# Second attention: each head's scores on one half of the array's rows, a second copy of the negated maxima, late scores last

## The reference

```
q = (x @ wq).reshape(b, s, H, HD)        # H = 32, HD = 16
k = (x @ wk).reshape(b, s, H, HD)
v = (x @ wv).reshape(b, s, H, HD)
q = _apply_rotary(q, cos, sin)
k = _apply_rotary(k, cos, sin)
scores = jnp.einsum('bqhd,bkhd->bhqk', q, k) * scale
scores = jnp.where(causal[None, None], scores, jnp.finfo(scores.dtype).min)
probs = jax.nn.softmax(scores, axis=-1)
out = jnp.einsum('bhqk,bkhd->bqhd', probs, v).reshape(b, s, d)
return out @ wo
```

## Time and profile before

| | before |
|---|---|
| median of 3 runs | 1991.2 us (1982.42 to 1991.51) |
| profiled execution, its own time | 1992.31 us |
| its span | 1990.6 us |
| mean granted TensorE clock | 0.984 |
| TensorE busy | 1926.6 us (97%) |
| weight loads busy | 1688.1 us (85%) |
| VectorE busy | 1504.9 us (76%) |
| ScalarE busy | 883.7 us (44%) |
| GpSimd busy | 908.0 us (46%) |

### The profile page before, as it was taken

One profiled execution on the slowest core, in us unless ns is written; L12 is line 12 of the kernel. 1 busy time (PEld: TensorE's weight loads), 2 busy tenths in 40 slices (PEclk: granted clock), 3 DMA queues, 4 the chain that ended last, 5 costly groups with the idle time before them and its releaser, 6 DMA issues.

```text
span 1990.6 us, 41276 instructions
## 1 busy us (share of the span) xinstructions
PE 1926.6 (97%) x13992; PEld 1688.1 (85%) x13992; DVE 1504.9 (76%) x2322; ACT 883.7 (44%) x2235; POOL 908.0 (46%) x872
## 2 busy tenths in 40 slices
PE   8999979999999999999999999988999989999998
PEld 3688869999999999999999999987888868888776
DVE  2577657887788788877887788888888457778886
ACT  1233334444444444444444444446554346666432
POOL 0133354444444444444444444454684557777111
PEclk9999989999999999999999999999999889999999
DMA  9577741111111111111111111411487754443121
GB/s 342 170 242 243 236 143 42 47 48 47 48 47 47 48 47 46 41 44 42 47 47 48 47 47 43 141 43 64 141 245 210 220 164 137 140 135 112 38 64 58
DMA packets 197085, 207.20 MB, mean 104 GB/s; under 512 B 18554, under 2 KB 167930, under 8 KB 195996
## 3 DMA queue, kind: packets, MB, share of 16 engines
q1 hardware_dynamic: 196156, 205.53, 33.5%
q10 hardware_dynamic: 864, 0.79, 0.1%
HBM read 126.43 MB, written 71.43 MB: 99 GB/s over the span
## 4 chain that ended last, share of the span: by engine, by line
PE 77%; issue 11%; DVE 5%; POOL 3%; SPq 2%; DMA 2%; ACT 1%; POOLq 0%; DVEq 0%; ACTq 0%
PE ps L1036 18%; PE ps L997 18%; PE ps L1011 7%; PE ps L1025 4%; PE ps L1048 4%; PE ps L2128 3%; PE ps L1020 3%; PE ps L2099 3%; PE ps L2557 2%; POOL k_rot L570 2%; PE ps L1806 2%; PE ps L2148 2%; PE ps L2521 2%; PE ps L1118 1%; PE ps L1814 1%
## 5 line engine op out<-in xcount | busy, mean ns | idle before, releaser
L1036 PE MATMUL ps<-wo,ot 128*128 (+1 forms) x1536 | 389.0, 402 | 0.0
L1036 PEld LDWEIGHTS ps<-wo,ot 128*128 128x128 f32 x1536 | 282.0, 190 | 60.3 <-issue 1.2
L997 PE MATMUL ps<-ht_hi,wq 128*128 (+1 forms) x2048 | 287.6, 283 | 5.2 <-DVE q_swap L869 5.2
L997 PEld LDWEIGHTS ps<-ht_hi,wq 128*128 128x128 f32 x2048 | 268.6, 192 | 11.1 <-DVE q_swap L869 5.4
L795 ACT ACTIVATE prob<-ps,neg_max 128x128 f32<-128x128 f32 (+1 forms) x512 | 208.3, 421 | 129.8 <-DVE neg_max L876 104.8
L954 POOL TENSOR_TENSOR q_rot<-q_rot,q_swap 128x512 f32<-128x512 f32 x128 | 165.2, 1291 | 198.2 <-DVE q_swap L869 193.7
L802 ACT ACTIVATE pt<-ps 128x512 fp32r<-128x512 f32 x192 | 107.9, 598 | 301.7 <-PE ps L1048 301.7
L949 POOL TENSOR_TENSOR prob<-prob,inv_sum 128x512 f32<-128x512 f32 x64 | 66.6, 1040 | 281.0 <-DVE inv_sum L885 281.0
L1993 DVE TENSOR_REDUCE f_neg_max<-ps 128x4 f32<-128x1024 f32 (+1 forms) x128 | 119.8, 954 | 80.4 <-PE ps L2099 80.4
L997 PE MATMUL ps<-ht_lo,wq 128*128 (+1 forms) x1024 | 165.0, 283 | 0.0
L1011 PE MATMUL ps<-pt,vv 128*128 128x512 f32 x576 | 144.1, 394 | 4.0 <-issue 3.8
(11 more groups left out here) (248 smaller groups left out, 4244.6 us busy)
## 6 DMA issues: line engine op xcount, KB each, us to landing
stack_dram<-e_part SPq DMA_DIRECT2D x192, 128.0 KB, 2.4
v_dram<-v_part SPq DMA_DIRECT2D x32, 512.0 KB, 5.7
k_dram<-k_part SPq DMA_DIRECT2D x64, 256.0 KB, 2.5
kk<-k_dram SPq DMA_DIRECT2D x128, 128.0 KB, 2.1
vv<-v_dram SPq DMA_DIRECT2D x128, 128.0 KB, 2.1
wmod<-in_wmod SPq DMA_DIRECT2D x12, 1024.0 KB, 11.9
f_q<-stack_dram SPq DMA_DIRECT2D x62, 192.0 KB, 2.6
f_k<-stack_dram SPq DMA_DIRECT2D x124, 96.0 KB, 2.5
```

The lines of the kernel that those rows point to most:

```text
L997: mm = nc.tensor.matmul(ps_q[j][:, e], w[:, c:c + HD0], r[:, bass.ds(u % B, 1), k].rearrange("p o s -> p (o s)"), start=(n == 0), stop=(n ...
L1036: mm = nc.tensor.matmul(ps_y[j][:], o[:, j, h * P:(h + 1) * P], w[:, bass.ds(at + h * D, D)], start=(n == 0), stop=(n == len(passes) - 1))
```

## The change

Each head's stack now has 52 rows, four rows of `own` and 48 of products, and lies whole in one half of the partitions: the even head of a pair at 0 to 51, the odd head at 64 to 115. No product needs zero rows any more. A score product uses 52 rows of one half, and the two heads of a pair (`e` = 0 and 1) write to different PSUM banks. The rows of `own` are stored once to the stacks in DRAM (16 DMAs of 128 KB at the start of the projections), and `load_unit` brings them with the rest, by four DMAs of 104 KB where there were three (192 and twice 96 KB).

The negated maxima must now stand in both halves. `negated_again` makes the second copy from the first, in SBUF, behind the exponentials. The order on TensorE is new: shifted scores first (first half of the keys, then second), then the early scores (`s0`) of unit v+2, and its late scores (`s1`) last before the values. The turned maxima now share bank 0 with `s1`. The output of a pair is made in two halves of 128 columns, in two steps. `warm` is gone. `begin` waits until the last product of the rotation has been read, since `s0` lies in banks 2 and 3, and step 63 waits for the last exponentials ahead of its half of the output projection.

```diff
-M_ROW = 96
+ROWS1 = 4 + 3 * HD1
+PLACE1 = (0, 2, 1, 3)
...
+        sp.wait_ge(own_out, 2)
+        for n in range(2):
+            for b in range(B):
+                sp.dma_start(keep.stacks1[n][b, :, 0:HU1].rearrange("h r s -> h r s"), f32(rows1[n][:])).then_inc(own_kept, 16)
...
-            for i, tile in enumerate(keep.k1):
-                if i == 0:
-                    routed_exp(act, 1)
-                nc.scalar.activation(tile[:], own[:], ACT.Identity).then_inc(own_out, 1)
+            nc.scalar.activation(rows1[0][:], own[:], ACT.Identity, scale=0.0).then_inc(own_out, 1)
+            routed_exp(act, 1)
+            nc.scalar.activation(rows1[1][:], own[:], ACT.Identity).then_inc(own_out, 1)
...
-    sp.dma_start(f32(keep.q1[slot][0:2 * rows]), src[0]).then_inc(keep.qk1_in[slot], 16)
-    for e in range(2):
-        half = slice(rows * e, rows * (e + 1))
-        sp.dma_start(f32(keep.k1[slot][half, e:HU1:2]), src[1][half]).then_inc(keep.qk1_in[slot], 16)
+    for t, stack in ((keep.q1, keep.stacks1[0]), (keep.k1, keep.stacks1[1])):
+        src = stack[bass.ds(u // 8, 1), bass.ds(u % 8 * HU1, HU1)].rearrange("o (i e) r s -> (o e) r i s", e=2)
+        for e in range(2):
+            sp.dma_start(f32(t[slot][64 * e:64 * e + ROWS1, 0:2]), src[e]).then_inc(keep.qk1_in[slot], 16)
...
+    max_rows = keep.ps[0:HU, 0, 0:S]
+    s0 = keep.ps[:, 2:4, 0:S].rearrange("p e (i k) -> p e i k", i=2)
+    s1 = keep.ps[:, 0:2].rearrange("p e (i k) -> p e i k", i=2)
+    t1 = keep.ps[:, 2:4, S:2 * S].rearrange("p e (i k) -> p e i k", i=2)
+    t0 = keep.ps[:, 4:6].rearrange("p e (i k) -> p e i k", i=2)
...
-            for t, sc in ((1, s1), (0, s0)):
-                dve.wait_ge(s_done, 2 * u + 2 - t)
+            for t, sc in ((0, s0), (1, s1)):
+                dve.wait_ge(s_done, 4 * u + 2 * t + 2)
...
+        def negated_again(u, slot):
+
+            act.wait_ge(m_out, 2 * u + 1)
+            nc.scalar.activation(q[slot][64:64 + HU], f32(q[slot][0:HU]), ACT.Identity).then_inc(m_out, 1)
...
+            for j, (p, sc) in enumerate(((prob0, t0), (prob1, t1))):
+                act.wait_ge(t_done, 4 * u + 2 * j + 2)
+                if j and at < U - 2:
+                    act.wait_ge(smax, 2 * u + 5)
...
+    def score(pe, slot, t, e, i):
+
+        rows = slice(64 * e, 64 * e + ROWS1)
+        return nc.tensor.matmul((s0, s1)[t][:, e, i], q[slot][rows, i, t * P:(t + 1) * P],
+                                k[slot][rows, i, 0:P * (t + 1)], start=False, stop=True, skip_group_check=True)
...
+    def scores_late(pe, u, slot, first=False):
+
+        if not first:
+            pe.wait_ge(m_out, 2 * u - 1)
+        for e in range(2):
+            put_mask(1, e)
+        for e in range(2):
+            score(pe, slot, 1, e, 0)
+        for e in range(2):
+            score(pe, slot, 1, e, 1).then_inc(s_done, 1)
...
+            pe.wait_ge(keep.p_mul, 4 * B + 1)
+            mask_early()
+            scores_early(pe, 0, 0)
+            scores_late(pe, 0, 0, first=True)
...
+            if 0 <= at < U:
+                pe.wait_ge(m_out, 2 * v + 2)
+                if at > 0:
+                    pe.wait_ge(p_exp, 2 * v)
+                if at < U - 2:
+                    mask_early()
+                shifted_near(v, slot)
+                shifted_far(v, slot)
             if 0 <= at < U - 2:
-                scores(pe, v + 2, (slot + 2) % NS, at, 1)
-            if 0 <= at < U:
-                shifted(v, slot, at)
+                scores_early(pe, v + 2, (slot + 2) % NS)
             if -1 <= at < U - 2:
-                scores(pe, v + 2, (slot + 2) % NS, at, 0)
-            if at == 1:
-                warm()
+                scores_late(pe, v + 2, (slot + 2) % NS)
+            if at == U - 1:
+                pe.wait_ge(p_exp, 2 * U)
```

More of the change, by code:

```diff
@@ L1201, in projections1 @@
     delta = at("e_delta", [P, TT, D], low(6))
-    own = at("f_own", [P, HU1, S], keep.tokens_at)
+    own = at("f_own", [P, S], keep.tokens_at)
+    rows1 = [at(f"f_rows{n}", [P, S], keep.tokens_at + (1 + n) * S * 4, F32R) for n in range(2)]
     spacer = small("d_spacer", [P, 1])
@@ L2005, in step @@
                 maxima(v + 2, slot % 2)
-            if 2 <= at and slot % 2:
-                output((v - 3) // 2, (slot + 1) // 2 % 2)
+            if 3 <= at and slot % 2:
+                output((v - 3) // 2, (slot + 1) // 2 % 2, 0)
+            if 4 <= at and not slot % 2:
+                output((v - 4) // 2, slot // 2, 1)
             if at >= TAIL:
                 side(dve, at - TAIL)
-        dve.sem_inc(o_out, 2)
+        dve.sem_inc(o_out, 4)
         dve.wait_ge(keep.p_done, 6 * B - 2)
@@ L2021, in vector @@
         rest(dve, step)
-        output(PAIRS - 1, 1)
+        for t in range(TT):
+            output(PAIRS - 1, 1, t)
     def scalar(act, side):
@@ L2048, in step @@
                 exponentials(v, slot, at)
+            if -1 <= at < U - 1:
+                negated_again(v + 1, (slot + 1) % NS)
             if at in (0, 1):
                 load_unit(act, keep, NS + v, v)
-            if 4 <= at and not slot % 2:
-                high((v - 4) // 2)
+            if 5 <= at and slot % 2:
+                high((v - 5) // 2)
             if at >= TAIL:
@@ L2082, in step @@
                 add_blocks(v, slot)
-            if 5 <= at and slot % 2:
-                low((v - 5) // 2)
+            if 6 <= at and not slot % 2:
+                low((v - 6) // 2)
         steps(pool, step)
@@ L2088, in gpsimd, with put_mask, mask_early, scores_early @@
         low(PAIRS - 1)
[L2090 to L2102, removed]
+    def score(pe, slot, t, e, i):
+        rows = slice(64 * e, 64 * e + ROWS1)
+        return nc.tensor.matmul((s0, s1)[t][:, e, i], q[slot][rows, i, t * P:(t + 1) * P],
+                                k[slot][rows, i, 0:P * (t + 1)], start=False, stop=True, skip_group_check=True)
+    def put_mask(t, e):
+        mask = keep.mask_b[:].rearrange("p (o k) -> p o k", o=1).broadcast_to([P, 2, P])
+        nc.tensor.matmul((s0, s1)[t][:, e, :, t * P:(t + 1) * P], keep.ident_b[:], mask,
+                         start=True, stop=False, skip_group_check=True)
+    def scores_late(pe, u, slot, first=False):
[7 more added lines that the diff above has]
+            score(pe, slot, 1, e, 1).then_inc(s_done, 1)
+    def mask_early():
+        for e in range(2):
+            put_mask(0, e)
+    def scores_early(pe, u, slot):
+        pe.wait_ge(qk_in[slot], 64 * (u // NS) + 64)
+        for e in range(2):
+            score(pe, slot, 0, e, 0)
+        for e in range(2):
+            score(pe, slot, 0, e, 1).then_inc(s_done, 1)
     def turn_max(pe, u, first, at):
@@ L2752, in tables @@
     cos1, sin1 = (np.tile(t.T, (2 * P // HD1, 1)) for t in (np.cos(angle1), np.sin(angle1)))
-    own = np.zeros((P, 4, S), np.float32)
-    for h in range(4):
-        own[M_ROW + h, h] = 1.0
+    own = np.zeros((H1, HU1, S), np.float32)
+    for h in range(H1):
+        own[h, PLACE1[h % HU1]] = 1.0
+    own = own.reshape(P, S)
     def earlier(n):
```

87 lines of the change are left out of this document (38 added, 49 removed).

## The result

The changed kernel took 1972.3 us (median of six executions; five of them took 1970.3 to 1973.7) beside 1988.6 us for the kernel before: a ratio of 0.9919, 95% interval 0.9899 to 0.9938. It is faster by 0.8%. The sixth execution took 3070.7 us at a mean granted clock of 0.556 and is left out of the ratio; without it the median is 1971.5. The profiled execution took 1970.3 us for a span of 1968.6; that of before had 1992.3 and 1990.6.

The account below looks back on a forecast made before the run. TensorE alone was taken to bound the steady step of 3.787 us. Terms +2.0 - 4.8 + 1.0 - 1.0 - 7.3 + 1.2 + 1.4 = -7.5 us gave a 1984 us median, range 1973 to 2001.

Parts of the forecast that it names:

- Steps 2 to 11: Early steps with two waits on loads: nothing gained except one shorter half-clock step after each wait, together -1.0 us.
- Pairs: TensorE score products: two heads on different row halves share one slot, so 8 pairs take 0.90 us a step, not 1.80.
- the rival of unshared pairs: Each pair of score products costs two slots: loop 4.52 us, time about 2030 us; chance 0.10.
- Switches: TensorE changes between 128-row and 52-row products: three more a step at 0.20 us each, 0.60 us.
- The rival of cheap switches: Each switch on TensorE costs only 0.13 us: loop 3.41 us, time 1974 us; chance 0.20.
- The loop: Steady steps: turn, masks, switches, pairs and long reduction set 3.62 us a step; TensorE waits about 0.14; saves 7.3 us.
- What has to fit: Under 3.62 us a step: ScalarE's second copy (0.58) hidden, VectorE's half output 1.25, DMA share 0.53.
- Start, steps 0 and 1: Start +2.0 us; steps 0 and 1 at half clock 5.6 and 6.5 us, -4.8, with +1.0 for a later clock rise.
- The rival of the low clock: Without `warm` the clock rises three steps later: time 1992 us; chance 0.09.
- Steps 56 to 61: Near the stage's end VectorE needs 4.32 us a step where steps took 4.12: +1.2 us.
- dearer pairs: Score pairs cost a little more than a slot: 1995 us at 0.03 more, about 2002 at 0.05; chance 0.10.
- loads that set the step: More bytes in less time: steady steps stay at 3.79 us, time 1991 us; chance 0.09.

Follow-up runs that it names:

- e4: Changed kernel with TensorE's wait for the load of the unit two ahead put back ahead of the early masks and shifted products; 1978.0 us.
- e1: Changed kernel with the two products of one row half issued one after the other in each group of four; 1972.5 us.
- e2: Changed kernel with one extra far shifted product in every second step, ahead of the late scores; 1975.8 us.
- e3: Changed kernel with one extra product in every second step, behind the late scores, at the head of the products with values; 1972.9 us.
- e5: Changed kernel with the 16 warm products of 512 columns put back into step 1; 1978.6 us.
- e7: Changed kernel with a pair's output made whole, 256 columns in odd steps, in place of one half in each step; 1980.0 us.
- e6: Kernel before without the 16 warm products of 512 columns in step 1; 1984.8 us.
- e14: Kernel before with a pair's output made in halves, one in each step; 1989.3 us.
- e9: Changed kernel with the loads of the next stage's weights, gates and tables spread in eight pieces behind rounds 2 to 9; 1963.5 us.
- e10: Kernel before with the loads of the next stage's weights spread in eight pieces behind rounds 2 to 9; 1978.6 us.
- e13: Changed kernel with all score and shifted products reading rows 0 and on, so none are of opposite halves; 2042.9 us.

## Why the prediction was wrong

The mechanisms were mostly right. The median is 11.7 us below the forecast, and the span fell by 14.4 us more than I had, by the table of stretches: 5.8 in steps 2 to 11, 3.8 in the steady steps, 3.0 in steps 0 and 1, 2.3 in steps 56 to 61, and -0.5 elsewhere.

*Steps 2 to 11, the step that failed.* "A load is issued when its predecessor has been used, and weights go ahead of it, so what TensorE gains it waits longer. I count nothing, apart from one step at half clock after each wait". That made -1.0; the two traces have -6.8. The first late load's DMA was indeed as long as before, 9.8 us. But I had looked only at the waiting and not at what is queued behind it. The change moves the wait for the unit two ahead from in front of the shifted products to behind them. Of the work that a late load holds up, the shifted products and the masks ahead of them were gone, and what was left was shorter: 2.4 us at the first, of which e4, which moved only the wait back, took 1.4. By the starts of the turned maxima in the timelines, the next turn comes 4.2 us behind the first landing and 3.2 to 4.2 behind the second in the changed kernel, e1, e2, e3, e5 and e7, 6.0 to 6.6 and 6.2 to 6.6 in the kernel before, e6 and e14, and 5.6 at both in e4. e9 and e10 took the late loads away from both kernels, and with them the difference in steps 2 to 11 fell from 6.8 to 1.7. The size is less sure than the step: kernels with the changed wait have 45.7 to 49.3 in steps 2 to 11, those with the old one 51.3 to 52.5.

*Pairs.* One slot a pair was right: with the surpluses below taken off, the eight pairs take 1.84 - 0.44 - 0.51 = 0.89 us. Without opposite halves (e13) the products take the 0.90 a step more that the rival of unshared pairs had. The Trainium skill, page TensorEngine Tiling (Array Packing), section Key Properties, says that different tiles can load and multiply in parallel. The 0.88 us a step by which e13 is longer at full clock agree.

*Switches.* Three at 0.20 were counted, 0.60. In the single records of step 27 the masks-to-shifted change has a surplus of 0.20, early scores to late masks 0.11, late masks to late scores 0.20, so 0.51. Masks, switches and pairs were 0.44 + 0.60 + 0.90 = 1.94 in the forecast and are 0.22 + 0.61 + 0.22 + 0.32 + 0.47 = 1.84 in the chain. This is the difference of 3.62 to 3.53, and makes 44 x 0.09 = 3.8 us. The rival of cheap switches (0.13 each, a loop of 3.41) gave the nearest time, 1974, but its size is wrong at two switches of three; its time was met by luck: it saved 16.7 us in the steady steps, where 11.1 came, and other terms made up for that.

*The loop.* Right: the chain, e2 and e3 show it, with TensorE idle 0.13 a step for 0.14 forecast.

*What has to fit.* The second copy takes 0.63 for 0.58 and is hidden. A half output takes 0.95 + 0.29 = 1.24 for 1.25. I had costed the halves as what fits; e7 shows that they are a condition. The DMA share is 0.53, as forecast.

*Start, steps 0 and 1.* Start +1.9 for +2.0. Step 0 takes 4.04 and not 5.6: the granted clock was at 1.00 until 1578.02, so its chain up to the early scores ran at 2.4 GHz, and I had put all of it at the lower level. Where the clock falls here differs from trace to trace: at 0.5 from 1575.56 on in the kernel before, at 1.00 through both steps in e14, whose work in them is the same. Step 1 takes 5.97 for 6.5. The +1.0 for a clock that rises later was not needed: it rose at 1588.26, and at 1589.21 before, and e5 finds no gain in steps 2 to 11 from `warm`. The rival of the low clock falls.

*Steps 56 to 61.* VectorE sets them, as forecast, but at 23.64 / 6 = 3.94 and not 4.32. Its timeline:

```profile
1797.70 1.81 DVE L1991 TENSOR_REDUCE f_neg_max<-ps 128x4 f32<-128x512 f32 x2
1799.43 0.94 DVE L1997 RECIPROCAL f_inv_sum<-ps 128x128 f32<-128x128 f32 x1
1800.40 0.29 DVE L2000 TENSOR_TENSOR turned_raw<-ps,f_inv_sum 128x128 f32<-128x128 f32 x1
1800.61 1.12 DVE L2457 TENSOR_TENSOR g_lo<-g_raw,g_w 128x512 fp32r<-128x512 f32 x1
1801.66 1.81 DVE L1991 TENSOR_REDUCE f_neg_max<-ps 128x4 f32<-128x512 f32 x2
```

Instructions that do not wait for each other start up to 0.08 before the one ahead ends: both reductions together need 1.73 (1797.70 to 1799.43) and not 0.69 + 1.22, the half output 1.18 (to 1800.61) and not 1.36. I had added whole durations. The kernel before with half outputs (e14) needs 22.7 there for 24.7, so the whole outputs had cost it time in this stretch; that gain I had not seen at all.

*The rest* was +2.0 for +1.4. The rivals of unshared or dearer pairs and of loads that set the step fall with the steady step of 3.533.

## What to carry to other kernels

Where a stream of transfers is late at a few places, an edit that moves the wait relative to other work on the waiting engine is worth about what now stands in front of the wait, once for each late transfer: look at the chain from the landing to the next step, not at the length of the wait. When the work of the bounding engine gets shorter, ask of each other engine whether its longest piece fits between two deadlines: here whole outputs on VectorE cost nothing in the steady steps at 3.79 us and nearly their entire gain at 3.53. And loads for a later stage belong between those of the present one in small pieces: that gave 8 to 11 us more here (by the spans 7.9, by the medians 8.8, by the ratios 11).

## What the runs showed of the hardware

- The two row halves of TensorE each went on by themselves: in e1 a product of the second half started 7 ns behind the first one of the first half, ahead of the product that stands between them in the program, and a steady step was 3.545 us for 3.533.
- Going over from scores of 128 columns to masks had a surplus of 0.11 us, from masks to products of 52 rows 0.20.
- In e13 the granted clock kept falling to 0.5 and rising again between 1698 and 1896 us, although TensorE was hardly idle. The window from 1700 to 1890 us has 188.2 us busy of 190 at a mean of 0.83:

```profile
1700.00:1890.00 190.00, 188.22 (x2010) 135.89 (x2002) 116.76 (x154) 116.46 (x174) 107.01 (x130) 0.83 0.36 106
```

  The changed kernel had 1.00 in its steady steps with 150.18 of 155.80 busy. What took the clock down in e13, whose busy products were on half of the rows, no run settles.
- With spread loads (e9, e10) the granted clock stayed at 1.00 from 1590 to beyond 1800 us; without, it fell about both waits for a load.
